# Output copies beside Gelu, squares and gate later, row scatters behind the last pair; in the expert part roots ahead of scatters

## The reference, cut to what matters

```python
o_inter = qg @ Hst;  A = (qg @ kg.T) * causal;  o_intra = A @ v      # gated linear attention, per chunk
rms = sqrt(mean(o * o, -1) + EPS)                                    # over the 64 columns of a head
o = o / rms * g_norm_w * g * sigmoid(g);  out1 = o @ Wo
probs = softmax(q @ k.T * scale);  x = layer_norm(src + (probs @ v) @ Wo + bo)
e = remainder(floor(x @ router_w + router_b), 4)
y = relu(x @ W1[e] + b1[e]) @ W2[e] + b2[e]
out2 = layer_norm(x + y);   result = x1 + out1 + out2
```

## Time and profile before

| | us |
|---|---|
| median of 3 runs | 2942.77 |
| lowest and highest | 2938.26, 2957.74 |
| profiled execution, its own time | 2948.69 |
| its span, first to last instruction | 2946.9 |

### The profile page before, as it was taken

The page is one execution under the profiler, slowest core; times in us unless marked ns, Lnnn a source line. Parts: engine busy times, 40 slices in busy tenths (PEclk is TensorE's granted clock), DMA queues, the critical chain, the costliest instruction groups (busy, mean ns, idle before and its releaser), DMA issues. The chain is left out here.

```text
span 2946.9 us, 44459 instructions
## 1 busy us (share of the span) xinstructions
PE 2449.9 (83%) x14254; PEld 1682.9 (57%) x14254; DVE 1962.4 (67%) x3710; ACT 1340.6 (45%) x1914; POOL 589.1 (20%) x630
## 2 busy tenths in 40 slices
PE   3999999999998058788888888888888888887485
PEld 3788888888887045455544455445444454442474
DVE  3888888888885205667766676767766676651365
ACT  1444444444443013365555555555656555544232
POOL 0211211211111000112122221212121212211265
PEclk9999999999998576799999999999999997765698
DMA  2121121121121332244223432343233412210562
GB/s 76 36 76 43 39 75 43 39 75 43 39 71 40 101 101 86 78 116 120 74 77 107 125 93 65 92 125 105 68 95 107 125 51 62 76 41 15 182 196 81
DMA packets 158731, 240.02 MB, mean 81 GB/s; under 512 B 21080, under 2 KB 116905, under 8 KB 150064
## 3 DMA queue, kind: packets, MB, share of 16 engines
q1 hardware_dynamic: 153136, 226.23, 25.5%
q0 software_dynamic: 5504, 12.63, 1.2%
HBM read 145.38 MB, written 94.95 MB: 82 GB/s over the span
## 5 line engine op out<-in xcount | busy, mean ns | idle before, releaser
L1485 DVE TENSOR_REDUCE c_row_max<-b_psum 128x2 f32<-128x1024 f32 x512 | 624.8, 1220 | 384.4 <-PE b_psum L1200 381.9
L1334 ACT ACTIVATE c_prob<-b_psum 128x1024 f32<-128x1024 f32 x512 | 525.1, 1026 | 429.0 <-PE b_psum L1218 420.1
L1218 PE MATMUL b_psum<-c_cq,c_ck 25*128 25x512 f32 x1024 | 278.5, 540 | 133.8 <-ACT c_prob L1334 128.5
L1200 PE MATMUL b_psum<-c_bk,c_bq 24*128 24x512 f32 x1024 | 281.2, 545 | 53.1 <-DVE c_row_max L1485 42.2
L1228 PE MATMUL b_psum<-c_prob,c_v_aug 128*32 128x512 f32 x2048 | 313.0, 688 | 0.1
L1218 PEld LDWEIGHTS b_psum<-c_cq,c_ck 25*128 25x128 f32 x1024 | 102.3, 196 | 325.3 <-ACT c_prob L1334 236.9
L315 PE MATMUL a_psum<-a_yT_hi,a_w_hi 128*128 128x512 f32 x512 | 205.9, 402 | 7.0 <-issue 4.7
L315 PE MATMUL a_psum<-a_yT_hi,a_w_lo 128*128 128x512 f32 x512 | 202.7, 396 | 0.0
L315 PE MATMUL a_psum<-a_yT_lo,a_w_hi 128*128 128x512 f32 x512 | 202.6, 396 | 0.0
L1090 PE MATMUL b_psum<-c_g_hi,b_f_hi 128*128 128x512 f32 x256 | 121.1, 473 | 67.8 <-DMA c_g_lo<-g_scratch 63.3
L464 DVE TENSOR_TENSOR_SCAN a_st_sb<-a_decay,a_kv_sb 128x512 f32<-128x512 f32 x128 | 156.8, 1225 | 4.4
(11 more groups left out here) (300 smaller groups left out, 5563.0 us busy)
## 6 DMA issues: line engine op xcount, KB each, us to landing
g_scratch<-a_g_hi SPq DMA_DIRECT2D x16, 1024.0 KB, 4.0
g_scratch<-a_g_lo SPq DMA_DIRECT2D x16, 1024.0 KB, 6.9
c_g_hi<-g_scratch SPq DMA_DIRECT2D x16, 1024.0 KB
c_g_lo<-g_scratch SPq DMA_DIRECT2D x16, 1024.0 KB
stack_scratch<-c_qk_hi SPq DMA_DIRECT2D x256, 64.0 KB, 1.6
d_wt<-expert_scratch SPq DMA_DIRECT2D x19, 834.0 KB
c_bq<-stack_scratch SPq DMA_DIRECT2D x128, 96.0 KB
c_bk<-stack_scratch SPq DMA_DIRECT2D x128, 96.0 KB
```

Source lines behind the costliest of these rows:

```text
L1200: mm = nc.tensor.matmul(psum[:, MAX + x, :], bq[r, j, cut(t)], bk[r, j, :], start=True, stop=True)
L1218: mm = nc.tensor.matmul(psum[:, SCORE + x, :], ck[r, j, cut(kb)], cq[r, j, :], start=True, stop=True)
L1334: nc.scalar.activation(prob[:, i % 4, :, :], psum[:, SCORE:SCORE + 2, :], ACT.Exp, scale=DH1 ** -0.5).then_inc(S["exp"], 1)
L1485: nc.vector.tensor_reduce(row_max[:, t, at:at + 3:2], psum[:, MAX:MAX + 2, :], AX.X, ALU.max).then_inc(S["row_max"], 1)
```

## The change

PE and SP issue the same instructions in the same order as before. In `attention`, ACT's step `gz` is cut in three (`gzexp` behind pair 1, `gzln` behind pair 2). In pair 4 `aoT` goes ahead of `gz2`, in pair 14 `A` ahead of `front2`. The copies of the output banks no longer wait for squares: DVE makes both in pair 21, and ACT squares the copy in SBUF in pair 24, ahead of `gate` and `O2`. `scatter` goes from pair 27 to the end of pair 31, behind `r1b`. In `experts`, POOL takes the root of group k+1 ahead of the scatters of group k, and DVE's multiplication by the root is a function `write` that comes behind `begin` of the next group.

```diff
@@ attention_order
     put(1, "C2", "pv", STEPS - 1)
+    put(1, "A1", "gzexp")
     put(2, "C2", "ao", HPG - 1)
+    put(2, "A1", "gzln")
...
+    put(4, "C2", "aoT", HPG - 1)
     put(4, "A1", "gz2")
-    put(4, "C2", "aoT", HPG - 1)
...
-    put(27, "C2", "scatter")
     put(9, "C2", "r1_ld")
+    put(14, "A1", "A", 0)
     put(14, "A0", "front2")
-    put(14, "A1", "A", 0)
...
-    put(22, "A1", "ocopy", 0)
-    put(22, "A1", "gate")
-    put(23, "A1", "ocopy", 1)
+    put(21, "A1", "ocopy", 0)
+    put(21, "A1", "ocopy", 1)
+    put(24, "A1", "osquare", 0)
+    put(24, "A1", "osquare", 1)
+    put(24, "A1", "gate")
     put(24, "A1", "O2")
...
     put(31, "A1", "r1b")
+    put(31, "C2", "scatter")
@@ attention, ACT
-                    elif kind == "ocopy":
-                        turn_on(f"O{i}")
-                        act.wait_ge(S["o_n"], upto(stage, 1, 0))
-                        o = bank(f"O{i}").rearrange("p (t d) -> p t d", t=2)
-                        nc.scalar.activation(o_n[:, 2 * i:2 * i + 2, :], o, ACT.Square).then_inc(S["o_square"], 1)
+                    elif kind == "osquare":
+                        act.wait_ge(S["o_ready"], upto(stage, 2, i + 1))
+                        act.wait_ge(S["A1_filled"], upto(stage, len(uses["A1"]), uses["A1"].index("oT1") + 1 - len(uses["A1"])))
+                        nc.scalar.activation(o_n[:, 2 * i:2 * i + 2, :], o_sb[:, 2 * i:2 * i + 2, :], ACT.Square).then_inc(S["o_square"], 1)
@@ attention, DVE
                     elif kind == "ocopy":
-                        dve.wait_ge(S["o_square"], upto(stage, 2, i + 1))
+                        turn_on(f"O{i}")
                         nc.vector.tensor_copy(o_sb[:, 2 * i:2 * i + 2, :],
...
                     elif kind == "O2":
-                        dve.wait_ge(S["o_ready"], upto(stage, 2, 2))
+                        dve.wait_ge(S["o_square"], upto(stage, 2, 2))
@@ experts, DVE
                 ins.then_inc(S["scaled"], 1)
+
+            def write(k):
+                x = xt[k % XB]
                 dve.wait_ge(S["scaled"], k + 1)
                 dve.wait_ge(S["rs"], k + 1)
...
                 begin(k)
+                if k:
+                    write(k - 1)
             end(GROUPS - 1)
+            write(GROUPS - 1)
@@ experts, POOL
-            for k in range(GROUPS):
+            def root(k):
                 pool.wait_ge(S["mv"], k + 1)
                 nc.gpsimd.tensor_tensor(rs[:, 0, :], mv[:, :, 1], eps[:, :], ALU.add).then_inc(S["rs_step"], 1)
                 pool.wait_ge(S["rs_step"], k + 1)
+                pool.wait_ge(S["out"], k)
                 nc.gpsimd.tensor_tensor(rs[:, 1, :], rs[:, 0, :], minus_half[:, 0:TILES], ALU.pow).then_inc(S["rs"], 1)
+
+            root(0)
+            for k in range(GROUPS):
+                if k + 1 < GROUPS:
+                    root(k + 1)
                 pool.wait_ge(S["token"], k + 1)
                 pool.wait_ge(S["out"], k + 1)
```

More of the change, by code:

```diff
@@ L1287, in rounds @@
                         nc.scalar.activation(z_log[:, :], bank("gz"), ACT.Abs, bias=col("gk_b2")).then_inc(S["z_abs"], 1)
+                    elif kind == "gzexp":
                         act.wait_ge(S["z_abs"], upto(stage, 1, 1))
                         nc.scalar.activation(z_log[:, :], z_log[:, :], ACT.Exp, scale=-1.0).then_inc(S["z_exp"], 1)
+                    elif kind == "gzln":
                         act.wait_ge(S["z_exp"], upto(stage, 1, 1))
@@ L1866, in end @@
             def end(k):
-                x = xt[k % XB]
                 dve.wait_ge(S["y"], k + 1)
@@ L1882, in end @@
                     dve.wait_ge(S[f"out_out{k % 2}"], 16 * TILES * (k // 2))
-                nc.vector.tensor_copy(token[:, k % 2, :], x[:, :, 2 * P]).then_inc(S["token"], 1)
+                nc.vector.tensor_copy(token[:, k % 2, :], xt[k % XB][:, :, 2 * P]).then_inc(S["token"], 1)
                 dve.wait_ge(S["mv"], k + 1)
```

## The result

| | before | after |
|---|---|---|
| median of the runs, us | 2947.09 (4 runs, 2938.26 to 2957.74) | 2864.11 (4 runs, 2860.88 to 2875.63) |
| ratio after/before | | 0.9724, 95% interval 0.9679 to 0.9769 |
| span of the profiled execution, us | 2946.9 | 2864.4 |
| granted clock, whole span | 0.894 | 0.904 |

The changed kernel is 2.8% faster: 2864 us, where 2872 was forecast. The spans differ by 82.5 us. By the distances of the same instruction in both traces: 74.2 us between the first and the last sum of squares of the 16 rounds of `attention`, 2.0 from there to the first token cast of `experts`, 5.3 from the first to the last token cast, 1.1 behind it.

The account below looks back on a forecast made before the run. PE's work, its gaps waiting for ACT or DVE, and low-clock stretches bound the round. 60 us in `attention` and 10.6 in experts, together 71 off 2948.7, gave 2877.7; against the median 2872 us, case range 2850 to 2895, wider 2832 to 2920.

Parts of the forecast that it names:

- Round start: Pairs 1 and 2, `gz` in three: 0.36 us of PE's gap, plus 1.6 us of low clock in ten loop rounds.
- Pair 4: `aoT` ahead of `gz2`: PE's 0.93 us wait goes, but the reduction of pair 5 is late next; 0, bounds 0 and 0.9.
- Pair 14: Mask ahead of `front2`: PE's whole mask wait in pair 15 goes, 1.9 us per round, lower bound 0.8.
- Pairs 21 to 25: Copies, squares, gate moved: the chain comes only one copy earlier, 0.7 us per round, bounds 0 and 1.36.
- my first rival: Clock falls elsewhere: a fall of the same size comes at another place in `attention`; 2912 us, chance 0.18.
- The round as a whole: One loop round of `attention`, 95.5 us before, was to take about 91 us.
- Expert part: DVE's token cast waits for scatters to land, replacing the root wait: 7.78 us per group against 8.37, 10.6 us won.
- 12.25 + L: Expert part's chain over two groups; L is the scatters' landing time, taken as 3.3 us from a store.
- 6.76 us per group: Expert part: with L under 1.3 us POOL itself bounds each group, 29 us won.
- The slower rival: Late exponential of pair 24 delays the reductions behind `o_n`; slower from 3.3 us of delay; 2973 us, chance 0.05.

Follow-up runs that it names:

- experiment 2: The kernel before, unchanged, in a second profiled execution: its loop took 974.6 us, against 955.5 in the first.
- Experiment 12: The changed kernel with three buffers in the expert part, o_n in pair 26, slots in pair 27, the gate's running sum in pair 5: ratio to before 0.9492.
- experiment 5: The kernel before with only both output copies in pair 21, squares from SBUF and the gate in pair 24: ratio to before 0.9993.
- 6: The changed kernel with the copies, squares and gate put back to their old places: ratio to before 0.9714, against 0.9724 for the changed kernel.
- 11: The changed kernel with three buffers in the expert part, o_n moved from pair 25 to 26 and the slots to pair 27: ratio to before 0.9601.

## Why the prediction was right, and where it was not

**The total.** Forecast 71 us, measured 83 by the medians of four runs each. It is right in part because errors cancel: the mask's term is 23 us too small, those of the copies and of the expert part together 12 to 15 us too large.

| part | forecast, us | alone, us (interval) |
|---|---|---|
| gate steps (0.36 x 15 + 1.6 x 10) | 21 | 22 (13 to 31) |
| aoT, scatter | 0 | scatter -7 (-17 to 3) |
| mask first (1.9 x 15) | 29 | 52 (40 to 65) |
| copies, squares, gate (0.7 x 15) | 11 | 2 (-8 to 12) |
| expert part | 11 | 5 by the trace; 8 (-1 to 17) |

The third column is one less the ratio, times the median of before in that comparison. The product of the five ratios is 0.974, so the parts add up to the whole (0.9724, 0.9679 to 0.9769).

**Round start.** In the trace the step is right to 0.1 us: the exponential of pair 4 comes 1.9 us earlier, 0.4 from the reduction of pair 2 and the rest from the clock behind it, for which experiment 2 has 1.5 us between rounds of one kernel, forecast 1.6. The fall does go with the gap, 47 rounds of 60 with it and 7 of 80 without, but not by the fixed count of ten rounds that one execution shows.

**Pair 4.** Right: the late next was the reduction, 0.93 us for 0.93. Experiment 12 shows what it took to get at it.

**Pair 14.** The mechanism is right for the wait: the whole of it went, xn takes 1.11, nothing else became late. The 0.2 us that the prediction let the moved scaling pay beside POOL don't show: its first instruction takes 0.34 us like the others. The term was mis-sized, 29 us for 52. It held the wait and no clock, because the profiled execution had no fall there in any round, where most others have one. The bound said "up to 1.9" for the wait; for the clock behind it I had given no bound at all.

**Pairs 21 to 25.** The step "only by one copy earlier, 0.7 us" is right in the trace, the chain at pairs 27 and 28 comes 0.74 us earlier. Its worth isn't: experiments 5 and 6 find none, alone and in company. In the long rounds of the changed kernel the stretch of 6.8 us in pairs 27 to 31 takes it back, which is my first rival for this part alone, the clock falls elsewhere. That it is so in general isn't shown: experiment 5 against the second execution of before has no more low time, and its runs show no gain all the same.

**The round as a whole.** Forecast 91.0, measured 88.8. The difference of 2.2 is not in any term. 1.5 of it is the late start, which the profiled execution of before had in each loop round, its second execution in three of ten, and no kernel with an edited `attention` in any. The other five rounds won 7 us together in these two traces where 15 were forecast.

**Expert part.** The chain is right, token cast to landing in place of the root, and two sizes were off. With L at 4.1 to 5.1 up to group 10, 12.25 + L is 16.35 to 17.35 for two groups, and the trace has 16.1 to 17.2 (10.79 + 5.30 to 11.85 + 5.30), on average 16.7 as before; the 5.3 us come from the last seven intervals, four of them behind the last loads, where L is 1.3 to 2.3. I took 3.3 from a store. And I took 8.37 for all 18 intervals of before, which sum to 148.05 and not 150.7. The estimate with the 2.0 us of the Trainium skill (DMA: Bandwidth & Descriptors, "Anatomy of one DMA — SWDGE (gpsimd) path") would have given 22 us won. The trace disagrees while loads run (3.7 to 5.1 us), and is nearer without them (1.3 to 3.9). The part in which POOL bounds, 6.76 us per group, looks borne out by the 6.80 of experiments 11 and 12, but by luck: PE is busy all the time there and POOL waits a little in each group. POOL's own sets can stand 6.4 us apart.

**The slower rival.** Its threshold of 3.3 us of delay leaves out the 1.9 us of the mask; with it, by the same reckoning, the round is slower from 5.2 us on. The sum of squares came no later: 12.1 us behind the reduction of pair 21, before 12.8.

**What stays open.** Why the clock falls behind the mask's wait in most rounds and in none of the one execution that I was shown; what the late start of pair 31 was, and why it is missing with every edit in `attention`; why the one profile of the last kernel has the fall at the start of every other round.

## What to carry to other kernels

Price a wait of the matmul engine together with the fall of its clock that may come behind it, and by several executions: one shows the falls of that execution alone, and the fall can cost more than the wait. Idle time of PE that is closed beside another gap may come back as time at the lower clock, so time each part alone and in company before it is kept. When an order change replaces one wait by another, ask which buffer the new one stands for: one more buffer here gave 20 us by the trace where the reordering had given 5, and then another engine, PE, bounded.

## What the runs showed of the hardware that I had not expected

- The same program had its low stretches at different places in two executions: in one the 4.5 us behind a wait of 1.96 us were at a granted clock of 0.50, in the other the stretch behind a wait of 1.94 us was at 1.00. Its loop took 955.5 us in one and 974.6 in the other.
- With a wait of 1.95 us the clock fell behind it in 45 of 60 rounds, without it in none of 80. A fall there cost 0.7 to 2.5 us.
- A microsecond at the lower of the two levels (1.2 GHz in place of 2.4) added 0.36 us to PE's busy time over the loop, by the line through 14 executions, not the half that I had reckoned. Products that run back to back do take nearly twice as long: 2.08 us for 1.16.
- In the changed kernel a scatter of 256 KB in four issues released its wait 1.3 to 5.1 us after its last issue, the long times while 834 KB loads ran. Without those loads the median was 2.1.
- Beside a multiplication of 1.19 us on POOL, one scaling on DVE took 1.22 us, where it takes 0.34 by itself.
